# A fused decoder layer: its three stages joined into one block, TensorE's attention loop written out, and the row maximum spread by ScalarE and subtracted by one product per bank

## The reference

```python
# 1 linear attention and feed-forward, twice a layer norm
x = x0 + out_proj((qf @ kv) / max(qf @ z, 1e-6))        # 16 heads of 8, features elu(.)+1
x = x + gelu(layer_norm(x) @ w1 + b1) @ w2 + b2
# 2 cross attention over the 77 context tokens, 16 heads of 8
q = (query @ Wq.T + bq); k = (key_value @ Wk.T + bk); v = (key_value @ Wv.T + bv)
attn = einsum('bhtd,bhnd->bhtn', q, k) * scale
attn = where(key_padding_mask, -inf, attn)
attn = softmax(attn, axis=-1)
out = einsum('bhtn,bhnd->bhtd', attn, v) @ Wo.T + bo
# 3 mixture of experts: 8 experts, top 2, capacity int(1.25*T/E) rows per expert and slot
probs = softmax(xf @ gate_w.T); top_p, top_i = top_k(probs, 2)
```

## Time and profile before

| | |
|---|---|
| median of 3 runs | 1084.15 us (1074.35 to 1092.88) |
| the profiled execution | 1086.21 us |
| its span, first to last instruction | 1084.4 us |
| PE busy, share of the span | 85% |
| DVE, POOL, ACT busy | 56%, 49%, 43% |
| stage 1, to the last write of X | 0 to 294.9 us |
| stage 2, to the last scatter | 301.5 to 807 us |
| stage 3 | 810 to 1084 us |

### The profile page before, as it was taken

The page is one execution under the profiler, slowest core; times in us unless marked ns, Lnnn a source line. Parts: engine busy times, 40 slices in busy tenths (PEclk is TensorE's granted clock), DMA queues, the critical chain, the costliest instruction groups (busy, mean ns, idle before and its releaser), DMA issues. The chain is left out here.

```text
span 1084.4 us, 27090 instructions
## 1 busy us (share of the span) xinstructions
PE 917.1 (85%) x9362; PEld 648.0 (60%) x9362; DVE 602.6 (56%) x1890; ACT 468.6 (43%) x721; POOL 526.3 (49%) x716
## 2 busy tenths in 40 slices
PE   3699999999759999989989999999618999999970
PEld 2466776677526666656656666666405776666750
DVE  5687787776335566666747676664411222244436
ACT  1256556556215555454535555444303443334420
POOL 3344444444522245454545555544552766666770
PEclk9699999999959999898979999997658999999995
DMA  4488000000000000010000000000002333344418
GB/s 121 137 327 326 14 0 0 0 0 1 1 18 8 8 18 28 22 29 18 17 9 14 13 13 13 13 9 9 9 24 81 93 91 106 103 126 141 130 56 310
DMA packets 49902, 66.51 MB, mean 61 GB/s; under 512 B 12662, under 2 KB 27813, under 8 KB 49824
## 3 DMA queue, kind: packets, MB, share of 16 engines
q1 hardware_dynamic: 38448, 52.14, 15.1%
q0 software_dynamic: 9216, 8.42, 2.7%
q10 hardware_dynamic: 2160, 4.86, 1.1%
HBM read 33.83 MB, written 42.09 MB: 70 GB/s over the span
## 5 line engine op out<-in xcount | busy, mean ns | idle before, releaser
L1446 POOL DMA_INDIRECT expert_out<-yo,token x160 | 156.1, 976 | 94.6 <-issue 72.5
L1064 ACT ACTIVATE PT<-psum,key_bias 77x2048 f32<-77x2048 f32 x64 | 125.6, 1963 | 149.2 <-PE psum L1160 148.5
L787 POOL DMA_INDIRECT dispatched<-z,idx x128 | 129.0, 1008 | 85.5 <-DVE idx L955 42.8
L1490 DVE TENSOR_TENSOR h<-psum,act_g 128x512 f32<-128x512 f32 x80 | 55.3, 691 | 151.9 <-PE psum L1555 151.8
L846 DVE TENSOR_REDUCE top_score<-psum 128x8 f32<-128x616 f32 x128 | 101.8, 796 | 67.5 <-PE psum L1143 65.6
L1140 PE MATMUL psum<-Kb,qT 32*128 32x308 f32 x512 | 107.2, 495 | 1.7 <-DVE top_score L846 1.7
L1157 PE MATMUL psum<-qT,Kb 32*77 32x128 f32 x2048 | 92.3, 295 | 5.5 <-issue 5.5
L1526 ACT ACTIVATE act_g<-psum 128x512 f32<-128x512 f32 x80 | 47.8, 597 | 89.4 <-PE psum L1555 89.4
L1567 PE MATMUL psum<-down,h 128*128 128x128 f32 x640 | 79.1, 277 | 0.8 <-DVE h L1490 0.8
L1555 PE MATMUL psum<-xT,gate 128*128 128x512 f32 (+1 forms) x192 | 77.1, 531 | 0.8 <-ACT xT L1511 0.8
L1567 PEld LDWEIGHTS psum<-down,h 128*128 128x128 f32 x640 | 75.6, 194 | 2.1 <-DVE h L1490 1.7
(11 more groups left out here) (162 smaller groups left out, 1775.0 us busy)
## 6 DMA issues: line engine op xcount, KB each, us to landing
dispatched<-zeros SPq DMA_DIRECT2D x40, 258.0 KB, 2.8
xin<-dispatched SPq DMA_DIRECT2D x40, 258.0 KB, 3.8
expert_out<-zeros SPq DMA_DIRECT2D x32, 256.0 KB, 2.1
X<-in_x SPq DMA_DIRECT2D x16, 256.0 KB, 2.7
yb<-expert_out SPq DMA_DIRECT2D x16, 256.0 KB, 3.8
Y<-expert_out SPq DMA_DIRECT2D x7, 512.0 KB, 8.9
out<-Y ACTq DMA_DIRECT2D x7, 512.0 KB, 6.4
expert_out<-yo,token POOLq DMA_INDIRECT x160, 2.2
```

The lines of the kernel that those rows point to most:

```text
L787: pool.indirect_dma_start(xg, bass.IndirectOffsetOnAxis(ap=idx[par][:, t, k:k + 1], axis=0), z4[par][:, t, :], None, bounds_check=ROWS - 1 ...
L1064: nc.scalar.activation(PT[j % 2][:], T.rearrange("p a c -> p (a c)"), ACT.Exp, bias=key_bias[:, bass.ds(b, 1)]).then_inc(s["PT_ready"], 1)
L1446: pool.indirect_dma_start(yt[slot], bass.IndirectOffsetOnAxis(ap=token[i][:, t:t + 1], axis=0), yo[i][:, t, :], None, bounds_check=P * B - ...
```

## The change

There are four parts to it.

1. **One block.** All three stages are in one block; the barriers are gone. Stage 2 hands functions `between` to stage 1, which calls them at places inside its turns 13 to 17, and there each engine does the first work of stage 2: the layer norm of groups 0 and 1, queries, keys and values of group 0, all scores of batches 0 and 1, turn_top(0) and MT_side(0). `rest` begins with waits for stage 1's last work and then runs the groups from 0. The banks are dealt out anew for this: T has banks 4 to 7, pv 3, misc 2 (before: 2 to 5, 6, 7). `masked` is gone: the mask stays 0 or 1, and the -3e38 stands in `first_row`; `mask_rows` casts the bytes per group. SyncE loads the later constants ahead of the mask and the zeros, and loads the first expert's weights once stage 1 is over instead of behind a barrier.
2. **TensorE's groups written out.** Only on TensorE: all groups of stage 2 are written out; the other engines keep their loop.
3. **`MT_side`** makes four copies of the transposed maxima instead of one, each multiplied by a column of `minus_spread` (-1 in the rows of head h and its rest, else 0), so that slot h of MT holds only what belongs to slot h.
4. **`shifted`** adds that with one product of 512 columns per bank, ones times MT, instead of four of 128.

```diff
-        linear_attention_and_ffn(nc, d, X, ident, block_mask, head_mask, neghalf, psum, banks, xg, yt, c)
-        cross_attention_and_routing(nc, d, X, ident, neghalf, psum, banks, xg, W, c)
-        experts_and_combine(nc, d, X, ident, psum, banks, xg, yt, W, out)
...
+        @block.tensor
+        def _(pe):
+            between, rest = attend["tensor"](pe)
+            mix["tensor"](pe, between)
+            rest()
+            experts["tensor"](pe)
...
-            pool.tensor_scalar(later["masked"][:], later["mask"][:], -3e38, None, ALU.mult).then_inc(s["masked_ready"], 1)
...
                 for h in range(HB):
                     for q in range(NQ):
                         nc.tensor.matmul(T[:, q, h * P:(h + 1) * P], Kb[par][rows_of(q), h, j * S2:(j + 1) * S2],
-                                         qT[par][rows_of(q), j * P:(j + 1) * P], start=True, stop=False)
-                    for q in range(NQ):
-                        last = nc.tensor.matmul(T[:, q, h * P:(h + 1) * P], minus_sel[rows_of(q), h, :], MT[rows_of(q), :],
-                                                start=False, stop=True)
-                        if h == HB - 1:
-                            last.then_inc(s["T_ps"], 1)
+                                         qT[par][rows_of(q), j * P:(j + 1) * P], start=(h == 0), stop=False)
+                for q in range(NQ):
+                    nc.tensor.matmul(T[:, q, :], ones[rows_of(q), 0:S2], MT[rows_of(q), :, :].rearrange("p h n -> p (h n)"),
+                                     start=False, stop=True).then_inc(s["T_ps"], 1)
...
-                nc.scalar.activation(MT[:], MT_ps, ACT.Copy).then_inc(s["MT_ready"], 1)
+
+                for h in range(HB):
+                    last = nc.scalar.activation(MT[:, h, :], MT_ps, ACT.Copy, scale=minus_spread[:, h:h + 1])
+                last.then_inc(s["MT_ready"], 1)
...
+            def between(g, place):
+                if not isinstance(g, int):
+                    return
+                if (g, place) == (NG - 2, "end"):
+                    pe.wait_ge(sems["a"]["later_loaded"], sems["later"])
+                    pe.wait_ge(sems["a"]["KV_ready"], NG)
+                    nc.tensor.matmul(misc[:, 0:P], bv_cols[:], wo[:], start=True, stop=True).then_inc(s["bias_ps"], 1)
+                if (g, place) == (NG - 1, "down01"):
+                    pe.wait_ge(s["bias_ready"], 1)
+                    t3(0)
+                if (g, place) == (NG - 1, "turn_y"):
+                    queries(0)
+                if (g, place) == (NG - 1, "out"):
+                    pe.wait_ge(s["qT_ready"], 1)
+                    keys(0, 0)
+                if (g, place) == (NG, "down01"):
+                    pe.wait_ge(s["Kb_ready"], 1)
+                    values(0, 0)
+                if (g, place) == (NG, "down3"):
+                    pe.wait_ge(sems["a"]["y_ready"], NG)
+                    scores(0, 0, 0, 0, 0)
+                if (g, place) == (NG, "up01"):
+                    scores(0, 0, 0, 0, 1)
+                if (g, place) == (NG, "end"):
+                    pe.wait_ge(s["V_ready"], 1)
+                    t3(1)
+                    scores(0, 0, 1, 1, 0)
+                    pe.wait_ge(s["z3T_ready"], 2)
+                    turn_top(0, 0)
+                if (g, place) == (NG + 1, "down3"):
+                    scores(0, 0, 1, 1, 1)
+
+            def rest():
+                pe.wait_ge(sems["a"]["x_out"], NG)
+                pe.wait_ge(sems["a"]["h_ready"], FC * NG)
+
+                for g in range(0, NG + 3):
+                    steps(g, g % 2)
...
+            sp.wait_ge(a["x_out"], NG)
+            sp.wait_ge(a["zeros_stored"], sems["zeros"])
             load_weights(0, 0, 0)
+            for par in (0, 1):
+                sp.wait_ge(b[f"scattered{par}"], 16 * G4 * K2 * NG // 2)
             load_x(0, 0, 0)
```

More of the change, by code:

```diff
@@ L478, in turn @@
             def turn(g):
+                between(g, "start")
                 if group(g - 1):
@@ L496, in _, with tensor @@
             turns(act, turn)
[L498 to L499 removed]
+        def tensor(pe, between):
             def t1(g):
```

244 lines of the change are left out of this document (155 added, 89 removed).

## The result

The changed kernel takes 1099.95 us (median of 20 runs, 1082.96 to 1124.62) beside 1085.68 for the kernel before (20 runs on the same chip, 1072.85 to 1103.41): a ratio of 1.0115, 95% interval 1.0069 to 1.016. It is a little slower. The time lies in the range, but the forecast was no change (-1 us) and +14 came, by a mechanism that the sum had left out, as the experiments show. The profiled execution took 1101.86 us, 15.7 more than that of before.

A forecast was written before the change was run, and what follows sets the result against it. TensorE was taken to bound stage 2, dependences the joint of stages 1 and 2. Terms -23.5 - 2.7 - 1 - 1 + 27 = -1.2, taken off the 1084.15 us median, gave 1083 us, range 1061 to 1104.

The forecast's parts named there:

- The joint of stages 1 and 2: Barrier and mask go, work moves into stage 1; first exponential at 305.0 instead of 328.55: -23.5 us (ends -17, -28.5).
- The two new waits: End of stage 1: queries wait for VectorE's copy, about 1.2 us; layer norm waits behind two groups' statistics, 2 us.
- The joint of stages 2 and 3: Weight loads move beside stage 2 and no barrier follows; token rows asked for sooner: -2.7 us (ends -2.3, -4).
- The joints as a price: Gains at both stage joints, -23.5 and -2.7 us, entered in the sum as gains of the whole kernel.
- TensorE written out: Stage 2 on TensorE: at most 0.2 us for each of 12 groups formerly in the loop: -1 us (ends 0, -2.4).
- `shifted`: Long products per bank take 1.13 to 1.16 us a batch against 1.16: -1 us (ends -2, +3).
- `MT_side`: Four ScalarE copies make MT 0.90 us later; TensorE stalls 1.92 us a group: +27 us (+10 to +54).
- the copies are dear: Rival: MT 1.38 us later stalls TensorE behind `weigh`, 1110 us; decides from about 1.3 us of delay; chance 0.1.
- clock: not counted in the sum: More lower-level clock time in stage 2, from added TensorE idling, got no term in the sum, only a rival.
- rival "the clock": TensorE idles 3.8 instead of 1.9 us a group; if clock falls come twice as often, +23, 1106 us; chance 0.15.

The follow-up runs named there:

- e7: Changed kernel with one plain MT copy, four short products per bank and TensorE's groups back in the loop; 1082.71 us, ratio 0.998.
- e9: Kernel before with only TensorE's groups of stage 2 written out; 1085.7 us, ratio 0.9981.
- e8: Changed kernel with one plain MT copy and four short products per bank, a repeat run in the second comparison; 1054.73 us, ratio 0.9613.
- e18: Changed kernel with one plain MT copy, long products, and five transposes ahead of the wait for o; repeat on the slower chip, 1091.55 us, ratio 0.9538.
- e17: Changed kernel with one plain MT copy, short products, and five transposes ahead of the wait for o; repeat on the slower chip, 1100.88 us, ratio 0.9612.
- e14: Changed kernel with small products ahead of each MT wait and five transposes ahead of the wait for o; slower chip, 1114.5 us, ratio 0.9653.
- e13: Changed kernel with one plain MT copy, long products, and five transposes ahead of the wait for o; slower chip, 1093.12 us, ratio 0.9443.
- e5: Changed kernel with its four MT copies kept and each long product cut into four of 128 columns; 1103.76 us, ratio 1.0198.
- e10: Changed kernel with small unread products on TensorE ahead of each wait for MT; 1085.28 us, ratio 0.9989.
- e11: Changed kernel with one plain MT copy, short products, and five transposes ahead of the wait for o at j=1; 1043.5 us, ratio 0.9593.
- e12: Changed kernel with one plain MT copy, short products, and two extra unread copies ahead of MT's; 1043.08 us, ratio 0.962.
- e1: Changed kernel with one plain MT copy and four short products per bank, first run; 1053.51 us, ratio 0.9646.
- e16: Kernel before with five transposes of the identity ahead of the wait for o at j=1; slower chip, 1154.71 us, ratio 1.0114.
- e15: Changed kernel with one plain MT copy, short products, five transposes ahead of the wait for o, and TensorE's loop; slower chip, 1100.6 us, ratio 0.9532.

## Why the prediction was wrong, point by point

**The joint of stages 1 and 2: right in itself.** First exponential at 304.66 (forecast 305.0), the clock at 1.00 from 268 on. The two new waits are there: 0.94 us for z3T ahead of queries (forecast 1.2), and 2.63 instead of 1.03 for the layer norm behind the statistics (forecast 2 more). ScalarE's row, with the first `MT_side` before it:

```profile
298.85 1.14 ACT L1148 ACTIVATE MT<-psum,minus_spread 128x128 bf16<-128x128 bf16 x4 [0.82 <-PE psum L1232]
300.01 1.28 ACT L1133 ACT_TABLE_LOAD   x1
304.66 1.96 ACT L1133 ACTIVATE PT<-psum,key_bias 77x2048 f32<-77x2048 f32 x1 [3.37 <-PE psum L1244]
```

**The joint of stages 2 and 3: right in kind, too small.** 4.1 us at the issue of the token rows, the upper end of the term; from the last exponential to the end 6.6.

**The joints as a price: -26 put down, -3 measured where the loop stays (e7 against before).** Of e7's earlier start nothing is left, since its stage 2 is 25 us longer than that of before (463.2 and 438.2): eight waits for instructions instead of two, and the clock. The prediction took a gain at the joint for a gain of the kernel.

**TensorE written out: wrong for the kernel it stands in.** The term was -1. In the kernel before it is within -9 to +4 (e9). In the joined kernel it is -28 (e7 against e8), since there the loop has 20 us of waits for instructions and the falls behind them. I had compared plain groups only. The two errors cancel: joints and writing out come to -31 together, where 27 were put down, and that sum is near by luck.

**`shifted`: right in sign.** It gives 0.05 us a batch, 3 us, where 1 was put down (end -2); e18 and e17 show 6 in stage 2. The start of the last product lies 0.955 us behind that of the first, with short ones 1.163. But the pieces of the sum were wrong: from the first of the four long ones to the next piece it is 0.325 us, not 0.21 to 0.24 (with short ones 0.165 from the first of the last four), so the long ones cost more than was put down for them, and what is gained lies ahead of them. The Trainium skill (TensorE: Matmul & The Clock Gate, Part 3) gives 3.07 times; the estimate by it, 0.28 us for the four, is nearer to 0.325, but the term made from it (+3 to +4 in the prediction, +2.6 by its own 4 x 0.23 + 0.28 against 1.16) has the wrong sign.

**`MT_side`: the direct part right.** 1.36 us of new stalls a group against 1.92, on the engine that was named, and less than forecast at every j. 27 were put down for the stalls alone, and 21.4 measured (e14, e13), some 4 of them the clock's. In the rival "the copies are dear" the bound was set wrong: by the prediction's own terms the stalls outweigh the 26 us of the joints from about 0.9 us of delay on, not from 1.3.

**The failed step is "clock: not counted in the sum".** The stalls raise TensorE's idle time in stage 2 from 29 to 42 us, and the lower level rises by 74 us; at the 0.45 us lost per us of the prediction that is 33 us. The whole price of the copies is 49 us by the medians of e5 and e8 (63 by their ratios) where 27 stood. That these stalls bring it is shown by e5 against e8 (240 and 152 us by all runs) and by e10, where work in the stalls takes back 52 of the 233 us. With both waits filled the copies bring hardly any of the clock down (e14 and e13: 145 and 136 us), so it is not the copies by themselves. e11 adds little to that, since e12 does as well without filler. When the clock falls, and why e10 keeps 181, stays open. The rival "the clock" had the mechanism, the size (twice as often; it was 2.4 times) and the place; I gave it 0.15 and left it out of the sum because the trace of before showed no cause for its falls. It did show one for two of the five: the waits at the head of a round. The other three, the one at 439 that I had looked at among them, stay without a cause.

The parts, by medians: joints and writing out -31 (e8; 27 put down), copies +49 (e5 against e8; 27), long products -4 (changed against e5, on another chip; 1), together +14. By the ratios: -42, +63 and -9, together +12. They add up by the way they are formed. The copies' part is what the forecast missed by; that the time still lies in the range owes something to the cancelled errors of the joints and the writing out.

## What to carry to other kernels

Where TensorE bounds a stage, a stall can cost its own length and as much again by the clock, as here: look at the share of the lower level in the trace of before, and put the clock into the sum, not among the rivals. One profile is not enough to tell it: take the mean clock of all runs. A delay was free within the slack and dear beyond it: MT 0.34 us later cost nothing, 0.87 later 49 us. A gain at one place is the kernel's only if the rest stays as it was: joining the blocks gave 25 us at the joint and 3 in all until TensorE's loop was written out. The version to keep is the joined and written-out kernel with one copy (e8, 1054.73 us, quicker than before by 2.8% by the medians and 3.9% by the ratio), and with filler at its longest wait it is at least no slower (e11, 1043.5 us).

## What the runs showed of the hardware that was not expected

- Idle times of 0.25 to 0.71 us, four in 28 us, in a TensorE that was 89% busy, went with 126 us at the lower clock level in stage 2 instead of 52; useless products in them brought it to 89 (by all runs, in the whole kernel: 233 instead of 189, and 181 with the products). The Trainium skill (TensorE: Matmul & The Clock Gate, A second HAM failure mode: psum-queue depth-cycling) tells of another kernel whose short idle times between groups made the clock swing; these traces agree in kind. Falls don't follow the sum of the idle time: e12 idled 31 us in stage 2 and was down 20, e1 idled 25 and was down 65.
- TensorE waited 2.2 to 3.0 us for its own instructions at the head of a round of a long loop, in three of the five kernels with TensorE's loop (e7, e16 and before: 8, 4 and 2 times), each time with a 16 KB transfer of instructions starting within 0.25 us of the wait's start; rounds without such transfers had no such wait, nor had straight code, which fetched all the time.
- A scale from a column makes a 128-column copy 366 ns instead of 273, 93 more; the 512-column copies of the earlier trace rows differ by 90. The scaled copies follow each other every 0.26 us, plain ones every 0.17.
- One chip ran the kernel before in 1155 to 1160 us, others in 1086. There a plain group of the filled kernels took 28.7 us where e11 takes 26.9, and what follows the last exponential 354 us (e17) instead of 312 (e11). In stage 2 of e17 there are 23 waits of up to 0.4 us for nothing that the profile shows, 7.3 us together, where e11 has none; e15 has such waits also where no instructions are transferred. The rest of the cause is open.
